# Soft mixture of experts on Trainium2: keeping the slot pass's logits in DRAM for the combine

## The chip, the cores and the metric

One core of one Trainium2 chip runs the whole program. The metric is the device time in microseconds (us) of one execution. Data are float32 unless a row says bf16.

## What is computed

The reference is a network of four residual layers over x (16 batches, 512 positions, 256 features). The first three (an attention over a context of 1601 keys, a low-rank feed-forward layer, a second attention) stand in the kernel's first stage, which the change leaves alone. The fourth is a soft mixture of 64 experts with 32 slots each, 2048 slots in all:

```python
def _L1_ffn_ref(x, phi, W, b):
    logits = jnp.einsum('bmd,dnp->bmnp', x, phi)
    dispatch = jax.nn.softmax(logits, axis=0)
    combine = jax.nn.softmax(logits.reshape(bsz, m, n * p), axis=-1).reshape(bsz, m, n, p)
    slots = jnp.einsum('bmd,bmnp->bnpd', x, dispatch)
    y = jnp.einsum('bnpd,nde->bnpe', slots, W) + b[None, :, None, :]
    out = jnp.einsum('bnpd,bmnp->bmd', y, combine)
    return out
x = x + _L1_ffn_ref(_layernorm(x, axis=-1), ...)
```

The same logits are used twice: through a softmax over the 16 batches (dispatch) and through a softmax over the 2048 slots (combine).

## The kernel before

`stage_two` runs after the first stage. It is written by hand for each engine: each has its list of instructions, and semaphores join them. The 2048 slots are cut into 16 slabs of 128 slots (4 experts), the 512 positions of a batch into 4 groups of 128 (QT). All of x, normalised and transposed (`xT`, 8 MB), and `phi` (2 MB) lie in SBUF.

**The slot pass.** A tile n is one slab and one group of positions, for all 16 batches: 128 positions on the partitions, 16 x 128 logits along the row, 1 MB, in one of 10 buffers of `disp`. There are 64 tiles.
- TensorE: `logits` (L1479) multiplies a quarter of a tile (4 batches) into a PSUM bank; ScalarE's `evacuate` (L1581) copies it to `disp`.
- VectorE: `front(n)` takes the maximum over the batches as a tree (L1651, L1654 to L1658), the maximum of each row (L1652), and subtracts the former in place (L1660); ScalarE's `exponent` (L1587) follows, then `back(n)` on VectorE sums and inverts (L1669 to L1679), and POOL's `normalise` (L1460) multiplies.
- TensorE: `slots(s, p)` (L1494) multiplies two batches of x (`xnb`, two buffers, loaded by SP one batch at a time at L1425) by the weights of slab s; ScalarE copies the result out (L1593), `experts` (L1509) multiplies by the experts' matrices, VectorE's `add_bias` (L1686) adds the bias, and ScalarE's queue stores two batches of y (L1599) to `y_d` in DRAM.

The order on TensorE is one step g for a slab and a pair of batches, 128 steps: a quarter of a tile of logits, `slots`, another quarter, `experts` of the step before. The logits run 6 tiles ahead, so the last 12 steps have none. Every slab SP also loads the next experts' weights (L1412, L1415) behind the load of batch 6.

**The combine.** The logits are not kept. For a block of one batch b and one slab c, 256 blocks in all, TensorE computes them again, this time with slots on the partitions and the 512 positions along the row:

```python
for k in range(2):
    mm(o, phi[:, k, c * P:(c + 1) * P], xT[:, b, k, :], start=(k == 0), stop=False)
mm(o, ones3[:, :], shift[b % 2], start=False, stop=True).then_inc(c_mm, 1)
```

The third matmul subtracts each position's maximum, given as three bf16 rows (`shift_rows`, L1535). ScalarE takes the exponential from PSUM (L1630), and two blocks later TensorE's `combine` (L1557) multiplies four groups of 128 positions by y, with a column of ones behind the 256 of y, which sums the denominators. After 16 slabs of a batch VectorE's `finish` takes four reciprocals (L1732) and adds the result to the residual (L1737), and ScalarE's queue stores the batch (L1637). SP loads y of a batch (L1431, 2 MB, in pieces of 1 KB) and its residual (L1435).

Of the kernel before, what the change touches and what calls it, by code (L numbers as in the profile page):

```python
# [12 lines left out]
P = 128  # L13
B, S, D = 16, 512, 256
NK = 1601
QT = S // P
# [1304 lines left out]
def stage_two(nc, w, x3_d, xn_d, xnT_d, y_d, out, ident, psum):  # L1321
# [9 lines left out]
    LAG = 2  # L1331

    with ExitStack() as st:
# [18 lines left out]
        ngr = sb("ngr", [P, QT, B])  # L1352
        ngp = sb("ngp", [P, QT, B, 3], BF16)
        ones3 = sb("ones3", [P, P], BF16)
        identb = sb("identb2", [P, P], BF16)

        flat = disp[:, :, :, :].rearrange("p r b n -> p (r b n)")
        TILE = B * SL
        ya = [flat[:, 4 * TILE:4 * TILE + NSL * (D + 1)].rearrange("p (c e) -> p c e", e=D + 1),
              flat[:, 4 * TILE + NSL * (D + 1):4 * TILE + 2 * NSL * (D + 1)].rearrange("p (c e) -> p c e", e=D + 1)]  # L1360
        x3 = [flat[:, 9 * TILE + i * QT * D:9 * TILE + (i + 1) * QT * D].rearrange("p (t d) -> p t d", d=D)
              for i in range(2)]
        ex = [flat[:, i * S:(i + 1) * S] for i in range(4)]
        shift = [flat[:, TILE + i * 256:TILE + (i + 1) * 256].bitcast(BF16) for i in range(2)]
        rc = sb("rc", [P, 2, QT])
# [21 lines left out]
        ng_ready = sem("ng_ready")  # L1387
        ng_tr = sem("ng_tr")
        shift_zero = sem("shift_zero")
        shift_ready = sem("shift_ready")  # L1390
        ones_made = sem("ones_made")
        y_in = [sem(f"y_in{i}") for i in range(2)]
        x3_in = [sem(f"x3_in{i}") for i in range(2)]
        c_mm = sem("c_mm")
        c_exp = sem("c_exp")
        o_mm = sem("o_mm")
        o_rc = sem("o_rc")
        o_ready = sem("o_ready")
        o_stored = [sem(f"o_stored{i}") for i in range(2)]
# [3 lines left out]
        def _(sp):  # L1403
# [14 lines left out]

            parameters(0)
# [10 lines left out]
            def values(b, c0, c1):  # L1430
                sp.dma_start(ya[b % 2][:, c0:c1, 0:D],  # L1431
                             y_d[b].rearrange("(p c) e -> p c e", c=NSL)[:, c0:c1, :]).then_inc(y_in[b % 2], 16)

            def residual(b):
                sp.dma_start(x3[b % 2], x3_d[b].rearrange("(p t) d -> p t d", t=QT)).then_inc(x3_in[b % 2], 16)  # L1435

            sp.wait_ge(ones_made, 1)
            for i in range(2):
                sp.wait_ge(y_stored[i], 16 * PAIRS * NSL // 2)
            for b in range(B):  # L1440
                if b >= 2:
                    sp.wait_ge(o_mm, NSL * (b - 1))
                values(b, 0, NSL)
                if b >= 2:
                    sp.wait_ge(o_stored[b % 2], 16 * (b // 2))
                residual(b)
            for i in range(2):
                sp.wait_ge(o_stored[i], 16 * (B // 2))

        @block.gpsimd  # L1450
        def _(pool):
            pool.memset(ones3[:, :], 0.0).then_inc(made, 1)
            pool.wait_ge(made, 1)
            pool.memset(ones3[0:3, :], 1.0).then_inc(made, 1)
            pool.tensor_copy(identb[:, :], ident[:, :]).then_inc(made, 1)

# [10 lines left out]
        def _(pe):  # L1467
# [61 lines left out]
            def shift_rows(b):  # L1529
                if b == 0:  # L1530
                    pe.wait_ge(ng_ready, 1)
                    pe.wait_ge(made, 3)
                tb = bank[3 - b % 2].bitcast(BF16)
                for t in range(QT):
                    last = nc.tensor.transpose(tb[0:3, t * P:(t + 1) * P], ngp[:, t, b, :], identb[:, :])  # L1535
                last.then_inc(ng_tr, 1)

            def scores(b, c):
                n = b * NSL + c
                if n >= 2:  # L1540
                    pe.wait_ge(c_exp, n - 1)
                o = bank[n % 2]
                for k in range(2):
                    mm(o, phi[:, k, c * P:(c + 1) * P], xT[:, b, k, :], start=(k == 0), stop=False)  # L1544
                if c == 0:
                    pe.wait_ge(shift_ready, b + 1)
                mm(o, ones3[:, :], shift[b % 2], start=False, stop=True).then_inc(c_mm, 1)  # L1547

            def combine(b, e):
                n = b * NSL + e  # L1550
                if e == 0:
                    pe.wait_ge(y_in[b % 2], 16 * (b // 2 + 1))
                    if b >= 1:
                        pe.wait_ge(o_ready, b)
                pe.wait_ge(c_exp, n + 1)
                for t in range(QT):
                    last = mm(bank[4 + t][:, 0:D + 1], ex[n % 4][:, t * P:(t + 1) * P], ya[b % 2][:, e, :],  # L1557
                              start=(e == 0), stop=(e == NSL - 1))
# [3 lines left out]
            shift_rows(0)  # L1562
            for n in range(B * NSL + LAG):
# [214 lines left out]
```

## Time and profile before

| what | value |
|---|---|
| device time, 3 runs | 6866.95 us median (6860.8 to 6872.46) |
| device time of the profiled execution | 6864.03 us |
| its span, from first to last instruction | 6862.2 us |
| first stage | up to 4646.84 us, where `xT` begins to load |
| load of phi and xT, then the slot pass | 4646.84 to about 5897 us |
| combine | about 5897 to 6862 us |
| busy: PE, DVE, ACT, POOL | 92%, 51%, 48%, 35% of the span |
| granted TensorE clock, mean | 0.975 of 2.4 GHz |
| DRAM traffic | 387.94 MB read, 151.28 MB written |

PE is TensorE, DVE VectorE, ACT ScalarE, PEld TensorE's weight loads, which run beside the matmuls. A float32 matmul stands as two records, a transpose or a bf16 matmul as one. The records' durations overlap, so the pace of a stretch is read from start to start. "SPq" and "ACTq" are the DMA queues of SP and ScalarE.

### The profile page before, as it was taken

Reading aid. Unit: us, or ns where it says so; the run is one execution under the profiler, and the core shown is the slowest. Engines: PE = TensorE matmul, PEld = TensorE weight load, DVE = VectorE, ACT = ScalarE, POOL = GpSimd, SP = SyncE. Lnnn points to the kernel's source line nnn. Section 1 sums busy time; section 2 is a strip of 40 time slices with the busy share of each in tenths; the row PEclk is TensorE's granted clock in tenths of the full one; section 3 lists DMA queues with packets and bytes.
Section 4 is the critical chain, followed back from the end, with each engine's and each line's share of the span. In section 5 each row is a group of like instructions: output and inputs, shape, how many; then the busy total and the mean of one; then the engine's idle time right before and its main releaser. Section 6 shows DMA issues by size and latency. Waiting matters only on the chain. (4 is left out here: it accounts for less than half of the span.)

```text
span 6862.2 us, 93027 instructions
## 1 busy us (share of the span) xinstructions
PE 6307.0 (92%) x35933; PEld 3091.1 (45%) x35933; DVE 3514.3 (51%) x6804; ACT 3263.7 (48%) x6001; POOL 2408.1 (35%) x2689
## 2 busy tenths in 40 slices
PE   3799999999999999999999999966999999999999
PEld 1223333333333333333333333226888888666666
DVE  3565665665656656656656566516666666000000
ACT  1366666666666666666666666522222222111111
POOL 4226436346355264363463552342222222000000
PEclk9799999999999999999999999968999999999999
DMA  2442332432432423314324324003444444311110
GB/s 64 77 76 57 67 76 56 73 69 63 76 71 55 84 57 66 78 55 73 69 63 76 70 53 75 6 16 135 157 167 154 158 162 163 121 56 56 49 56 31
DMA packets 364938, 546.09 MB, mean 80 GB/s; under 512 B 59824, under 2 KB 281984, under 8 KB 364240
## 3 DMA queue, kind: packets, MB, share of 16 engines
q1 hardware_dynamic: 321232, 498.18, 30.0%
q10 hardware_dynamic: 43264, 41.95, 1.8%
q8 instruction: 285, 4.67, 0.3%
q14 instruction: 157, 1.29, 0.1%
HBM read 387.94 MB, written 151.28 MB: 79 GB/s over the span
## 5 line engine op out<-in xcount | busy, mean ns | idle before, releaser
L1193 DVE TENSOR_REDUCE mx<-psum 128x1 f32<-128x401 f32 x4096 | 2212.9, 570 | 1615.7 <-PE psum L767 1606.6
L1038 ACT ACTIVATE probs<-psum 128x512 f32<-128x512 f32 (+1 forms) x3328 | 1910.6, 599 | 910.4 <-PE psum L789 907.3
L767 PE MATMUL psum<-kst,qst 96*128 96x401 bf16 x4096 | 1356.6, 343 | 192.5 <-DVE mx L1193 149.6
L789 PE MATMUL psum<-qst,kst 99*128 99x512 bf16 (+1 forms) x3328 | 1286.0, 387 | 49.9 <-ACT probs L1038 44.8
L800 PE MATMUL psum<-probs,vaug 128*17 128x512 f32 x6656 | 886.8, 605 | 0.0
L789 PEld LDWEIGHTS psum<-qst,kst 99*128 99x128 bf16 (+1 forms) x3328 | 328.8, 99 | 1178.5 <-ACT probs L1038 748.9
L767 PEld LDWEIGHTS psum<-kst,qst 96*128 96x128 bf16 x4096 | 402.7, 98 | 962.8 <-DVE mx L1193 756.3
L1460 POOL TENSOR_TENSOR disp<-disp,rz 128x2048 f32<-128x2048 f32 x64 | 294.7, 4605 | 905.5 <-DVE rz L1679 905.5
L1479 PE MATMUL psum<-phi,xT 128*128 128x128 f32 x4096 | 511.0, 279 | 39.1 <-DMA xT<-xnT_scratch 31.8
L1630 ACT ACTIVATE disp<-psum 128x512 f32<-128x512 f32 x256 | 152.8, 597 | 807.6 <-PE psum L1547 807.6
L1479 PEld LDWEIGHTS psum<-phi,xT 128*128 128x128 f32 x4096 | 479.0, 193 | 86.8 <-issue 79.1
L1494 PE MATMUL psum<-disp,xnb 128*128 128x128 f32 x4096 | 486.0, 276 | 27.0 <-POOL disp L1460 18.8
L1557 PE MATMUL psum<-disp 128*128 128x257 f32 x2048 | 487.5, 381 | 6.3 <-issue 4.0
L1494 PEld LDWEIGHTS psum<-disp,xnb 128*128 128x128 f32 x4096 | 470.6, 193 | 35.6 <-POOL disp L1460 19.6
L1544 PE MATMUL psum<-xT,phi 128*128 128x512 f32 x1024 | 485.1, 596 | 0.0
L1557 PEld LDWEIGHTS psum<-disp 128*128 128x128 f32 x2048 | 388.3, 190 | 143.5 <-issue 93.0
L644 POOL TENSOR_SCALAR rs<-mv 128x4 f32<-128x4 f32 x48 | 11.1, 231 | 1242.4 <-DVE mv L1245 1242.4
L725 PE MATMUL psum<-wkv,cT 128*128 128x512 f32 (+1 forms) x832 | 406.6, 611 | 12.7 <-ACT sq L1006 7.2
L1581 ACT ACTIVATE disp<-psum 128x512 f32<-128x512 f32 x256 | 152.1, 597 | 461.4 <-PE psum L1479 461.4
L1732 DVE RECIPROCAL rc<-psum 128x1 f32<-128x1 f32 x64 | 5.8, 153 | 599.9 <-PE psum L1557 599.9
L1686 DVE TENSOR_TENSOR ysb<-psum,be 128x512 f32<-128x512 f32 x128 | 88.5, 691 | 422.2 <-PE psum L1509 422.2
L1593 ACT ACTIVATE slT<-psum 128x512 f32<-128x512 f32 x128 | 76.4, 597 | 407.7 <-PE psum L1494 407.7
(197 smaller groups left out, 7556.2 us busy)
## 6 DMA issues: line engine op xcount, KB each, us to landing
xnb<-xn_scratch SPq DMA_DIRECT2D x256, 512.0 KB, 3.6
kst<-k_planes SPq DMA_DIRECT2D x384, 200.1 KB, 8.8
k_planes<-pl SPq DMA_DIRECT2D x96, 384.0 KB, 3.2
y_scratch<-ysb ACTq DMA_DIRECT2D x128, 256.0 KB, 3.3
disp<-y_scratch SPq DMA_DIRECT2D x16, 2048.0 KB, 9.2
vaug<-v_scratch SPq DMA_DIRECT2D x64, 442.0 KB, 4.6
v_scratch<-vst SPq DMA_DIRECT2D x48, 544.0 KB, 3.1
cin<-in_ctx SPq DMA_DIRECT2D x48, 512.0 KB, 3.8
```

Of the source, the lines that this page charges most:

```text
L725: last = mm(hb[0:m, :], cT[:, n % 2, k, a * P:a * P + m], wkv[:, k, :], start=(k == 0), stop=(k == 1))
L767: mm(to[:, 0:PW], qst[g][0:NP, j, t * P:(t + 1) * P], kst[g][0:NP, j, k0:k0 + PW], start=True, stop=True).then_inc(m_full, 1)
L789: mm(bank[S_BANK[n % 2]][0:m, :], kst[g][0:NR, j, c * P:c * P + m], qst[g][0:NR, j, :], start=True, stop=True).then_inc(s_full, 1)
L800: last = mm(bank[V_BANK][32 * j:32 * j + HV, :], vaug[0:m, g % 2, c, HV * j:HV * (j + 1)], probs[0:m, 4 * (k % 2) + j, :], start=(c == 0), ...
L1038: fn(probs[0:m, 4 * (k % 2) + j, :], bank[S_BANK[j % 2]][0:m, :], ACT.Exp, scale=float(HD) ** 0.5).then_inc(s_exp, 1)
L1193: v.tensor_reduce(mx[:, n % 2, u // 4, u % 4:u % 4 + 1], bank[M_BANK[r % 2]][:, 0:PW], AX.X, ALU.max).then_inc(m_free, 1)
L1460: pool.tensor_tensor(d, d, rz[:, n % 2, None, :].broadcast_to((P, B, SL)), ALU.mult).then_inc(normed, 1)
L1479: last = mm(bank[u % 4][:, a * SL:(a + 1) * SL], xT[:, 4 * q + a, k, t * P:(t + 1) * P], phi[:, k, s * SL:(s + 1) * SL], start=(k == 0), s ...
L1494: last = mm(bank[4 + n % 2][:, (2 * a + h) * SL:(2 * a + h + 1) * SL], xnb[:, a, t, h * P:(h + 1) * P], disp[:, (QT * s + t) % RING, b, :] ...
L1544: mm(o, phi[:, k, c * P:(c + 1) * P], xT[:, b, k, :], start=(k == 0), stop=False)
L1557: last = mm(bank[4 + t][:, 0:D + 1], ex[n % 4][:, t * P:(t + 1) * P], ya[b % 2][:, e, :], start=(e == 0), stop=(e == NSL - 1))
L1630: fn(ex[n % 4], bank[n % 2], ACT.Exp).then_inc(c_exp, 1)
```

## The change

Each tile's logits are stored to DRAM (`lg_d`, 64 MB in all) as soon as they are evacuated, pieces of 1 KB (128 slots of two neighbouring batches). VectorE's subtraction, which overwrites them, waits for that store. The combine works on a pair of batches, 32 blocks, in four units of 2 MB (4 slabs x 2 batches, rows of 4 KB). SP loads a unit into the place of `xT`, four buffers; the first two units go out in the last slab behind the load of batch 4, and 15/16 of batch 0's y behind that of batch 10. ScalarE exponentiates a unit in place, 8 instructions of 128 x 512 that subtract the maximum through the bias and sum the row (`accum_out`). TensorE transposes 4 groups of 128 x 128 of a block into a bank, VectorE copies the bank to `exT`, and two blocks later TensorE multiplies by y, now 256 columns wide. The two `scores` matmuls, the `ones3` matmul and the `shift` rows are gone. y and residuals have four buffers each; y is loaded in rows of 16 KB.

```diff
@@ SP
+            def logits_back(u):
+                if u >= 4:
+                    sp.wait_ge(tr_mm, 8 * (u - 3))
+                sp.dma_start(lgb[:, u % 4, :, :, :, :]..., lg_d[u // 4]...).then_inc(lg_in[u % 4], 16)
...
+                    if s == NSL - 1 and b == 4:
+                        sp.wait_ge(l_mm, 4 * TILES)
+                        for i in range(2):
+                            sp.wait_ge(lg_stored[i], 16 * (TILES // 2))
+                        logits_back(0)
+                        logits_back(1)
+                    if s == NSL - 1 and b == 10:
+                        for i in range(2):
+                            sp.wait_ge(y_stored[i], 16 * PAIRS * (NSL - 1) // 2)
+                        values(0, 0, NSL - 1)
+            for u in range(2, 4):
+                logits_back(u)
+            sp.wait_ge(sl_mm, B * NSL)
+            for i in range(4):
+                residual(i)
             for i in range(2):
                 sp.wait_ge(y_stored[i], 16 * PAIRS * NSL // 2)
+            values(0, NSL - 1, NSL)
+            for b in range(1, 4):
                 values(b, 0, NSL)
+            for p in range(PAIRS):
+                for h in range(4):
+                    if 4 * p + h + 4 < UNITS:
+                        logits_back(4 * p + h + 4)
+                if p + 2 < PAIRS:
+                    sp.wait_ge(o_mm, 2 * NSL * (p + 1))
+                    for b in (2 * p + 4, 2 * p + 5):
+                        values(b, 0, NSL)
+                    for b in (2 * p + 4, 2 * p + 5):
+                        sp.wait_ge(o_stored[b % 4], 16 * (b // 4))
+                        residual(b)
@@ TensorE
-            def scores(b, c):
...
-                for k in range(2):
-                    mm(o, phi[:, k, c * P:(c + 1) * P], xT[:, b, k, :], start=(k == 0), stop=False)
-                mm(o, ones3[:, :], shift[b % 2], start=False, stop=True).then_inc(c_mm, 1)
+            def transpose_back(n):
+                u, i, a = n // 8, n % 8 // 2, n % 2
+                if n % 8 < 2:
+                    pe.wait_ge(c_exp, 2 * QT * u + QT * (a + 1))
+                if n >= 4:
+                    pe.wait_ge(ex_ready, n - 3)
+                for t in range(QT):
+                    last = nc.tensor.transpose(bank[n % 4][:, t * P:(t + 1) * P], lgb[:, u % 4, t, i, a, :], ident[:, :])
+                last.then_inc(tr_mm, 1)
+            def combine(n):
+                p, e, a = n // (2 * NSL), n % (2 * NSL) // 2, n % 2
+                b = 2 * p + a
+                pe.wait_ge(ex_ready, n + 1)
+                if e == 0:
+                    pe.wait_ge(y_in[b % 4], 16 * (b // 4 + 1 + (b % 4 == 0)))
                 for t in range(QT):
+                    if e == 0 and a == 0 and p >= 1:
+                        pe.wait_ge(o_ready, 2 * QT * (p - 1) + 2 * t + 2)
+                    last = mm(bank[4 + t][:, a * D:(a + 1) * D], exT[n % 4][:, t * P:(t + 1) * P], ya[b % 4][:, e, :],
+                              start=(e == 0 and a == 0), stop=(e == NSL - 1), skip_group_check=True)
                 last.then_inc(o_mm, 1)
@@ ScalarE
+            def store_logits(n):
+                act.wait_ge(l_copied, 4 * n + 4)
+                if n >= 2:
+                    act.wait_ge(lg_stored[n % 2], 16 * (n // 2))
+                act.dma_start(lg_d[:, n % QT, :, n // QT, :]..., disp[:, n % RING, :, :]...).then_inc(lg_stored[n % 2], 16)
+            def weights(u):
...
+                        fn(d, d, ACT.Exp, bias=nm[:, t, b:b + 1], accum_out=sums[:, b % 4, t, h:h + 1]).then_inc(c_exp, 1)
+            for p in range(PAIRS):
+                for h in range(4):
+                    if 4 * p + h + 4 < UNITS:
+                        weights(4 * p + h + 4)
+                store_out(2 * p)
+                store_out(2 * p + 1)
@@ VectorE, front(n)
                 dve.wait_ge(front_step, base + 5)
+                dve.wait_ge(lg_stored[n % 2], 16 * (n // 2 + 1))
                 v.tensor_tensor(d, d, bm[:, None, :].broadcast_to((P, B, SL)), ALU.subtract).then_inc(shifted, 1)
@@ VectorE, combine
+            def copy_back(n):
+                dve.wait_ge(tr_mm, n + 1)
+                if n >= 4:
+                    dve.wait_ge(o_mm, n - 3)
+                v.tensor_copy(exT[n % 4], bank[n % 4]).then_inc(ex_ready, 1)
...
+            for n in range(BLOCKS + LAG):
+                if n < BLOCKS:
+                    copy_back(n)
+                if n % (2 * NSL) == 28 and n < BLOCKS:
+                    denominators(n // (2 * NSL))
+                if n >= 2 * NSL and n % (2 * NSL) == 1:
+                    finish(n // (2 * NSL) - 1)
```

TensorE in the middle of the combine, before (two blocks):

```order
L1544 MATMUL psum<-xT,phi 128x512 x2
L1547 MATMUL psum<-disp,ones 128x512
L1557 MATMUL psum<-disp 128x257 x4
L1544 MATMUL psum<-xT,phi 128x512 x2
L1547 MATMUL psum<-disp,ones 128x512
L1557 MATMUL psum<-disp 128x257 x4
```

and with the change (two blocks; `xT` is here the place of the logits that came back):

```order
L1562 MATMUL psum<-ident,xT 128x128 x4
L1574 MATMUL psum<-disp 128x256 x4
L1562 MATMUL psum<-ident,xT 128x128 x4
L1574 MATMUL psum<-disp 128x256 x4
```

Three matmuls of 512 columns have left each block, four transposes of 128 columns have come.

SP's queue over the last slab and the start of the combine, with the change (the loads into `xT` are logits, those of `y_scratch` are y, those of `x_scratch` residuals, 512 KB each):

```order
L1442 DMA xnb<-xn_scratch 128x1024 [waits sl_mm] x14
L1425 DMA xT<-logit_scratch 128x4x1024 [waits lg_stored1,lg_stored0,l_mm]
L1425 DMA xT<-logit_scratch 128x4x1024
L1442 DMA xnb<-xn_scratch 128x1024 [waits sl_mm] x6
L1430 DMA phi<-y_scratch 128x3840 [waits y_stored1,y_stored0]
L1442 DMA xnb<-xn_scratch 128x1024 [waits sl_mm] x5
L1425 DMA xT<-logit_scratch 128x4x1024 x2
L1434 DMA xnb<-x_scratch 128x1024 [waits sl_mm]
L1434 DMA xnb<-x_scratch 128x1024
L1434 DMA disp<-x_scratch 128x1024 x2
L1430 DMA phi<-y_scratch 128x256 [waits y_stored1,y_stored0]
L1430 DMA disp<-y_scratch 128x4096 x3
```

and the same stretch before:

```order
L1425 DMA xnb<-xn_scratch 128x1024 [waits sl_mm] x25
L1431 DMA disp<-y_scratch 128x16x256 [waits y_stored1,y_stored0,ones_made]
L1435 DMA disp<-x_scratch 128x1024
L1431 DMA disp<-y_scratch 128x16x256
L1435 DMA disp<-x_scratch 128x1024
```

Loads of 2 MB now stand between the loads of `xnb` of the last slab, and eight loads ahead of the last three of y.

VectorE at the border of two pairs, with the change: the eight additions to the residual stand between two copies of a block.

```order
L1749 COPY disp<-psum 128x512 [waits o_mm,tr_mm] x4
L1766 SCALAR_TENSOR_TENSOR xnb<-psum,rc,xnb 128x256 [waits x3_in1,x3_in0,o_mm]
L1766 SCALAR_TENSOR_TENSOR xnb<-psum,rc,xnb 128x256 x7
L1749 COPY disp<-psum 128x512 [waits o_mm,tr_mm] x27
```

## Rows read from the trace of the kernel before

**Rows 1.** The page's costliest groups: the two float32 matmuls of the combine.
```profile
L1557 PE MATMUL psum<-disp 128*128 128x257 f32 x2048 | 487.5, 381 | 6.3 <-issue 4.0
L1544 PE MATMUL psum<-xT,phi 128*128 128x512 f32 x1024 | 485.1, 596 | 0.0
```
**Rows 2.** Busy time by stretch (us, then PE, PEld, DVE, ACT, POOL; clock, DMA, GB/s): combine.
```profile
5907.00:6860.00 953.00, 945.75 (x3373) 607.38 (x3373) 38.55 (x143) 151.06 (x253) 0.00 (x0) 1.00 0.16 50
```
**Rows 3.** Timeline of PE in the combine (start, us, engine, line): one block.
```profile
6301.91 1.88 PE L1544 MATMUL psum<-xT,phi 128*128 128x512 f32 x4
6303.63 0.38 PE L1547 MATMUL psum<-disp,ones 128*128 128x512 bf16 x1
6303.85 1.90 PE L1557 MATMUL psum<-disp 128*128 128x257 f32 x8
6305.58 1.88 PE L1544 MATMUL psum<-xT,phi 128*128 128x512 f32 x4
```
**Rows 4.** Timeline of PE in the first stage: four float32 transposes, and what follows, twice.
```profile
3005.52 0.66 PE L748 MATMUL psum<-ident,kraw 128*128 128x128 f32 x4
3006.01 0.38 PE L789 MATMUL psum<-qst,kst 99*128 99x512 bf16 x1
...
3009.43 0.60 PE L748 MATMUL psum<-ident,kraw 128*128 128x128 f32 x4
3009.86 0.34 PE L767 MATMUL psum<-kst,qst 96*128 96x401 bf16 x1
```
**Rows 5.** Timeline of the slot pass, all engines, from one evacuation to a slab's start.
```profile
5163.27 0.60 ACT L1581 ACTIVATE disp<-psum 128x512 f32<-128x512 f32 x1 [1.19 <-PE psum L1479]
...
5170.60 2.29 DVE L1660 TENSOR_TENSOR disp<-disp,bm 128x2048 f32<-128x2048 f32 x1
...
5174.37 0.69 DVE L1686 TENSOR_TENSOR ysb<-psum,be 128x512 f32<-128x512 f32 x1 [1.40 <-PE psum L1509]
...
5178.77 4.54 POOL L1460 TENSOR_TENSOR disp<-disp,rz 128x2048 f32<-128x2048 f32 x1 [13.86 <-DVE rz L1679]
...
5185.33 3.74 PE L1494 MATMUL psum<-disp,xnb 128*128 128x128 f32 x32
```
**Rows 6.** Waits, 4740 to 5840 us: us in total, times, longest.
```profile
PE psum L1494 <- POOL disp L1460: 15.8, 1, 15.8
PE psum L1494 <- DMA xnb<-xn_scratch: 6.3, 9, 1.9
```
**Rows 7.** DMA, 4740 to 5840 us: ScalarE's queue (packets, MB, share); its stores, us to landing.
```profile
q10 hardware_dynamic: 31824, 30.68, 8.0%
...
y_scratch<-ysb ACTq DMA_DIRECT2D x118, 256.0 KB, 3.2
```
**Rows 8.** The chain of waits (start, us): the last of xT's load, 4 x 2 MB.
```profile
4646.84 24.39 DMA xT<-xnT_scratch
```
**Rows 9.** Timeline, all engines: from the last slab to the first combine.
```profile
5882.97 2.05 PE L1494 MATMUL psum<-disp,xnb 128*128 128x128 f32 x16 [0.41 <-DMA xnb<-xn_scratch]
...
5890.95 3.66 PE L1509 MATMUL psum<-we,slT 128*32 128x256 f32 x64
...
5897.61 0.62 SPq L1431 DMA_DIRECT2D disp<-y_scratch  x1
...
5906.86 3.02 PE L1557 MATMUL psum<-disp 128*128 128x257 f32 x8 [2.37 <-DMA disp<-y_scratch]
```
**Rows 10.** Busy time by stretch: the first combine matmuls.
```profile
5906.90:5909.70 2.80, 2.80 (x9) 2.26 (x10) 0.00 (x0) 0.00 (x0) 0.00 (x0) 0.64 1.08 353
```
**Rows 11.** Timeline: VectorE after one batch, and TensorE's last matmuls.
```profile
6264.84 1.66 DVE L1737 SCALAR_TENSOR_TENSOR disp<-psum,rc,disp 128x256 f32<-128x256 f32 x4
...
6851.35 5.37 PE L1557 MATMUL psum<-disp 128*128 128x257 f32 x24
```
**Rows 12.** Groups by line: a copy out of PSUM; the reading of an accumulated sum.
```profile
L1272 DVE COPY g_a<-psum 32x512 f32<-32x512 f32 x1 | 0.7, 678 | 1.1 <-PE psum L889 1.1
...
L1020 ACT ACTIVATION_READ_ACCUMULATOR kv1s<-psum,bkv 32x1 f32 x56 | 10.4, 185 | 0.0
```

More of the change, by code:

```diff
@@ L1450, in _ @@
+            for i in range(4):
+                sp.wait_ge(o_stored[i], 16 * (B // 4))
         @block.gpsimd
         def _(pool):
[L1452 to L1455, printed above, removed]
             def normalise(n):
@@ L1559, in combine @@
                 last.then_inc(o_mm, 1)
             pe.wait_ge(y_ready, PAIRS * NSL)
-            shift_rows(0)
-            for n in range(B * NSL + LAG):
-                b, c = n // NSL, n % NSL
-                if n < B * NSL:
-                    if c == NSL // 2 and b + 1 < B:
-                        shift_rows(b + 1)
-                    scores(b, c)
+            pe.wait_ge(l_copied, 4 * TILES)
+            for n in range(BLOCKS + LAG):
+                if n < BLOCKS:
+                    transpose_back(n)
@@ L1569, in _ @@
                 if n >= LAG:
-                    combine((n - LAG) // NSL, (n - LAG) % NSL)
+                    combine(n - LAG)
         @block.scalar
@@ L1587, in exponent @@
                 fn(d, d, ACT.Exp).then_inc(exped, 1)
+            def weights(u):
+                p, h = u // 4, u % 4
+                act.wait_ge(lg_in[u % 4], 16 * (u // 4 + 1))
+                if u == 0:
+                    act.wait_ge(nm_ready, 1)
+                if h == 0 and p >= 2:
+                    act.wait_ge(o_den, p - 1)
+                for a in range(2):
+                    b = 2 * p + a
+                    for t in range(QT):
+                        d = lgb[:, u % 4, t, :, a, :]
+                        fn(d, d, ACT.Exp, bias=nm[:, t, b:b + 1], accum_out=sums[:, b % 4, t, h:h + 1]).then_inc(c_exp, 1)
             def slots_out(g):
@@ L1604, in _ @@
                     evacuate(n, q)
+                store_logits(n)
                 if n >= 1:
@@ L1622, in _, with store_out @@
             store_y(NSL * PAIRS - 1)
-            for n in range(B * NSL):
-                act.wait_ge(c_mm, n + 1)
-                if n == 0:
-                    act.wait_ge(sl_mm, B * NSL)
-                if n >= 4:
-                    act.wait_ge(o_mm, n - 3)
-                fn(ex[n % 4], bank[n % 2], ACT.Exp).then_inc(c_exp, 1)
-                b, c = n // NSL, n % NSL
-                if b >= 1 and c == 6:
-                    act.wait_ge(o_ready, b)
-                    act.dma_start(out[b - 1].rearrange("(t p) d -> p t d", p=P), x3[(b - 1) % 2])\
-                        .then_inc(o_stored[(b - 1) % 2], 16)
-            act.wait_ge(o_ready, B)
-            act.dma_start(out[B - 1].rearrange("(t p) d -> p t d", p=P), x3[(B - 1) % 2])\
-                .then_inc(o_stored[(B - 1) % 2], 16)
+            def store_out(b):
+                act.wait_ge(o_ready, 2 * QT * (b // 2 + 1))
+                act.dma_start(out[b].rearrange("(t p) d -> p t d", p=P), x3[b % 4]).then_inc(o_stored[b % 4], 16)
+            for u in range(1, 4):
+                weights(u)
+            for p in range(PAIRS):
[4 more added lines that the diff above has]
+                store_out(2 * p + 1)
         @block.vector
@@ new lines, in finish @@
+            def finish(p):
+                dve.wait_ge(o_mm, 2 * NSL * (p + 1))
+                for b in (2 * p, 2 * p + 1):
+                    dve.wait_ge(x3_in[b % 4], 16 * (b // 4 + 1))
+                for t in range(QT):
+                    for a in range(2):
+                        i = (2 * p + a) % 4
+                        v.scalar_tensor_tensor(out=x3[i][:, t, :], in0=bank[4 + t][:, a * D:(a + 1) * D],
+                                               scalar=rc[:, i, t:t + 1], in1=x3[i][:, t, :],
+                                               op0=ALU.mult, op1=ALU.add).then_inc(o_ready, 1)
```

143 lines of the change are left out of this document (50 added, 93 removed).

## The prediction, made blind

> **What bounds the kernel now.** I read the groups by cost first, then the busy time by stretch, then the timeline of one block, of one slab's start and of the passage between the two passes, and last the waits and the DMA queues. TensorE is busy 945.75 of 953 us of the combine, at the full clock (1.00, the 2.4 GHz level) and with the DMA engines at 0.16 [rows 2]: nothing but TensorE's own work sets this stretch, and its other engines (DVE 38.55, ACT 151.06 us) could do much more. The two large groups are the recomputed scores, 485.1 us, and the product with y, 487.5 us [rows 1]. The slot pass is bound by TensorE as well: between 4740 and 5840 us it waits 15.8 us once for POOL, at the first slab, and 6.3 us in 9 pieces for loads of x [rows 6]. So what is removed from TensorE in the combine shortens the run, and what is added to the slot pass costs only where it breaks a cover.
>
> **The combine, block by block.** A block takes 3.67 us from start to start (6301.91 to 6305.58): scores 1.72, the bf16 matmul 0.22, the product with y 1.73 [rows 3]. The product stays, with 256 columns in place of 257: 1.72 us. The first two go, 1.94 us. Four float32 transposes come. In the first stage four of them take 0.49 and 0.43 us from their start to the next instruction's [rows 4]; I take 0.46. The trace shows no transpose right before a float32 product, whose weight loads are longer; the nearest bound from above is the slot pass, whose matmuls of the same 128 columns, as two records each, take 3.74 / 16 = 0.23 us [rows 5], four of them 0.93. I take 0.46, because that row is the same instruction on the same shape, and keep 0.93 as a rival. A block is then 2.18 us.
>
> Is that pace covered by the other engines? VectorE copies one bank per block; a copy of 512 columns out of PSUM takes 0.68 us [rows 12]. ScalarE's exponential over 512 columns takes 0.60 us, as its copy does [rows 5], with up to 0.19 us for reading the sum [rows 12]: 0.79 us. Both fit in 2.18 us. DMA: a pair of batches reads 8.4 MB of logits, 4.2 of y, 1.05 of residuals and writes 1.05, 14.7 MB in 32 blocks (70 us), or 210 GB/s. Loads in rows of 4 KB ran at 8.4 MB in 24.39 us [rows 8], 344 GB/s, so this is 43 us of transfer in 70. Four units are buffered, and SP asks for one as soon as the transposes of the unit before it in that buffer are done, three units (52 us) ahead of its use. SP does stop at the end of each pair for y's buffers and for the stores of the results, which stand on ScalarE's queue behind the last unit's exponentials: some 8 us of load, 6 of exponentials, 3 of store, so 17 us, and the next unit can't be asked for before 8 blocks (17 us) anyway. I cost that at nothing.
>
> **Borders of two batches.** Now VectorE does eight additions between two pairs where TensorE waits for bank after bank. Four take 1.66 us [rows 11], so the fourth bank is free 3.3 us after the last product, where TensorE, which has one block of transposes (0.46) and three quarters of a product (1.3) to do by then, wants it at 1.8: 1.5 us of stall, 7 times, 11 us.
>
> **The stores in the slot pass.** 64 stores of 1024 packets of 1 KB. The same form exists: y is stored in 1 KB pieces, 256 KB in 3.2 us, and ScalarE's queue used 0.080 x 1100 us x 16 engines for 31824 packets, 44 ns each [rows 7]. So 16 packets per engine are 0.7 us and 2.5 us are fixed; 64 packets are 2.8, and a store is 5.3 us, with up to 2.2 us more for two loads of x at the same time: 7.5 us. VectorE's subtraction now waits for it. The last evacuation ends at 5163.87 and the subtraction starts at 5170.60 [rows 5], 6.7 us later, so it starts 0.8 us late. Behind it on VectorE stands the bias addition, which waits 1.40 us for TensorE, and behind that the sums whose normalisation on POOL ends at 5183.31, 2.0 us ahead of the slab's first matmul [rows 5]. The cover is 3.4 us past the 6.7, so a store may take 10.1 us before TensorE feels it. Nothing for the wait; 0.5 us for each of 15 slabs where store, weights and loads of x collide, since TensorE already waits there for x [rows 6]: 7 us. Issuing a store takes about half a microsecond on ScalarE, which is idle half the time.
>
> The trace shows no store whose pieces lie 8 MB apart, as these do from pair to pair; y's, 2 MB apart, are the nearest. The Trainium skill, "DMA: Bandwidth & Descriptors", section "Latency and other measured facts", speaks against the change here: rows whose pitch is 4 or 8 MiB went at 103 GB/s where 512 KiB gave 207. By that page 1 MB is an estimated 10.2 us plus what is fixed, some 12.7 us, 2.6 us past the cover in each of 15 slabs, and the sum would be 39 us longer; no run here shows it.
>
> **The last slab and the start of the combine.** Four of SP's lines are moved past each other. Two units (4.2 MB, 12.2 us at 344 GB/s) go out ahead of x's batch 5, whose load has no spare in the last slab (a wait of 0.41 us there already [rows 9]) but is asked for 3 us later: 9 us of stall. y of batch 0 (2 MB, 5.7 us) ahead of batch 11: 3 us. Then, from the end of batch 13's slots at 5885.02 [rows 9], two units (12.2 us), four residuals (2.1 MB, 6.1), the rest of y of batch 0, and y of batch 1 (6.1) stand in one queue; the second block's product needs the last of these: 5885.0 + 24.9 + 2.5 fixed = 5912.5. Before, the first product started at 5906.86 [rows 9].
>
> **The sum**, on the profiled execution's 6864.03 us. The last product ended at 6851.35 + 5.37 = 6856.72 [rows 11]. Now 255 products (438.6 us) and 252 blocks of transposes (115.9) follow 5912.5: 6467.0, or -389.7. Borders +11, last slab +12, collisions +7. After a pause the matmuls run slower: the first product after the 2.37 us wait took 2.81 us in place of 1.73, at clock 0.64, between the 1.2 and 2.4 GHz levels [rows 9, 10]; nine pauses at half of that 1.1 us, +5. After the last product four more additions and one more store, less four reciprocals: +1.5. Together -353, so 6511 us. The median of the runs is 3 us above the profiled execution: **6514 us**. Between the small terms at nothing (with transposes at 0.43) and at double, this case spans 6483 to 6550.
>
> **The rivals.**
> A store slower than y's: if a packet took three times 44 ns, the store would be 8.4 + 2.5 + 2.2 = 13.1 us, 3.0 past the cover, 45 us in 15 slabs: 6559; at 15.8 us 6600. For it: 8 MB steps. Against: the same 1 KB packets in rows 7.
> Transposes at the pace of two records: +0.47 x 256 = 120 us, 6634. Against: rows 4.
> The combine bound by its loads: were 14.7 MB per pair to go at the slot pass's 160 GB/s, a pair would take 92 us in place of 71, 7 x 21 = 147: 6661. Against: that rate was what was asked for, and 344 was reached [rows 8].
> Slower than before: TensorE's clock stays at the 1.2 GHz level through the combine, because a fifth of its time is transposes and each border is a pause. Each block doubles, 256 x 2.18 = 558 us: 7072 us. It decides once 353 / 558 = 63% of the blocks run so. Against: the product with y fills four fifths of the time, and the clock came back to 1.00 within the next blocks after the drop [rows 2, 10]. The Trainium skill, "TensorE: Matmul & The Clock Gate", Part 4, says that transposes do not count as busy for the clock gate in the way matmuls do.
>
> **How the numbers follow.** The forecast 0.74, the slow store 0.11, two-record transposes 0.05, loads 0.05, the clock 0.04, and 0.01 for gain and losses that cancel. The range leaves out the last four: 6483 to 6600. About 0.2% (14 us) can be told from no change: faster 0.95, same 0.01, slower 0.04.
>
> **What would show it.** Blocks of 2.18 us from start to start at clock 1.00; no wait of TensorE in the combine but some 1.5 us at seven borders; stores landing in 5 to 8 us, and POOL's group still hardly waited for; a wait of about 9 us for x in the last slab; the second product at about 5925, with the earlier terms. Wrong: blocks above 2.3 us, POOL or DMA as what TensorE waits for at each slab, clock under 0.9, or the wait for y or logits at the start of each pair.

## The result, and the profile after

| | before | after |
|---|---|---|
| median | 6864.85 us (4 runs) | 6524.49 us (4 runs, 6520.53 to 6529.98) |
| ratio to before | | 0.9504 (95% interval 0.9488 to 0.9519) |
| span of the profiled execution | 6862.2 us | 6518.7 us |
| DRAM read / written | 387.94 / 151.28 MB | 455.04 / 218.39 MB |

The forecast was 6514 us in a range of 6483 to 6600. The run is 340 us shorter; 67 MB more are written and 67 MB more are read for it. From the start of `xT`'s load to the end of the span it is 1876 us where it was 2215.

The timeline of TensorE in the combine, one block (start us, us, engine, line), answers to [rows 3]:

```profile
6164.18 1.89 PE L1574 MATMUL psum<-disp 128*128 128x256 f32 x8
6165.91 0.60 PE L1562 MATMUL psum<-ident,xT 128*128 128x128 f32 x4
6166.34 1.89 PE L1574 MATMUL psum<-disp 128*128 128x256 f32 x8
```

From 6164.18 to 6166.34 is 2.16 us, where a block took 3.67. Four transposes take 0.43 us from their start to the product's, the lower of the two values of [rows 4].

Busy time by stretch in the combine (stretch, its length, then PE, PEld, DVE, ACT, POOL; clock, DMA, GB/s), as [rows 2]:

```profile
5960.00:6480.00 520.00, 514.30 (x2811) 445.70 (x2810) 185.97 (x305) 161.02 (x448) 0.00 (x0) 1.00 0.51 186
```

TensorE is still busy 99% of the stretch, at the 2.4 GHz level (1.00), with the DMA engines at half (0.51).

The border between two pairs of batches, TensorE and then VectorE:

```profile
6155.39 0.60 PE L1562 MATMUL psum<-ident,xT 128*128 128x128 f32 x4
6156.61 2.96 PE L1574 MATMUL psum<-disp 128*128 128x256 f32 x8 [0.62 <-DVE xnb L1766]
6159.41 0.60 PE L1562 MATMUL psum<-ident,xT 128*128 128x128 f32 x4
```

```profile
6155.59 3.23 DVE L1766 SCALAR_TENSOR_TENSOR xnb<-psum,rc,xnb 128x256 f32<-128x256 f32 x8 [1.04 <-PE psum L1574]
```

That block takes 4.02 us, 1.86 more than the others. Most of the stall does not stand as idle time: the product is drawn out from 1.73 to 2.80 us because it waits for one bank after another (`combine` has a wait for `o_ready` ahead of each of its four groups).

The DMA view of the slot pass, 4740 to 5850 us, answers to [rows 7]:

```profile
q10 hardware_dynamic: 92144, 91.50, 24.8%
...
logit_scratch<-disp ACTq DMA_DIRECT2D x58, 1024.0 KB, 5.3
y_scratch<-ysb ACTq DMA_DIRECT2D x118, 256.0 KB, 5.3
```

A store of 1 MB lands after 5.3 us at the median, the figure that was worked out from y's stores; the 64 stores took 4.7 to 6.9 us each; a packet took 0.248 x 1110 us x 16 / 92144 = 48 ns, against 44. y's stores, which share ScalarE's queue with the logits', went from 3.2 to 5.3 us.

Waits, 4640 to 5850 us (total us, times, longest), answer to [rows 6]:

```profile
PE psum L1520 <- POOL disp L1486: 15.8, 1, 15.8
PE psum L1520 <- DMA xnb<-xn_scratch: 13.7, 10, 2.4
...
DVE disp L1697 <- DMA logit_scratch<-disp: 0.3, 1, 0.3
```

VectorE hardly waits for a store and TensorE waits for POOL as before. TensorE's waits for x have doubled, from 6.3 us in 9 to 13.7 in 10. The longest of them, in the timeline of SP's queue and TensorE:

```profile
4832.74 0.32 SPq L1442 DMA_DIRECT2D xnb<-xn_scratch  x1
4833.11 0.93 SPq L1415 DMA_DIRECT2D we<-in_L_ffn_W  x1
4834.08 3.19 SPq L1418 DMA_DIRECT2D be<-in_L_ffn_b  x4
...
4837.31 10.59 SPq L1442 DMA_DIRECT2D xnb<-xn_scratch  x3
...
4844.31 3.23 PE L1520 MATMUL psum<-disp,xnb 128*128 128x128 f32 x16 [2.40 <-DMA xnb<-xn_scratch]
```

Issuing the weights and the four small loads of the biases keeps SP busy from 4833.11 to 4837.27; the next load of x is issued late, stands behind 1 MB, and shares the engines with y's store. This issuing is not typical: over the 15 slabs the five issues take 44 us in all, and took 40 in the kernel before. Behind this wait the matmuls are slow as well: 16 of them take 3.23 us where they take 2.05, and the granted clock from 4844.3 to 4850.0 is 0.70. Three of the ten waits (2.40, 2.32 and 1.90 us) are followed by such a stretch; the other seven are not, for example:

```profile
5665.51 2.05 PE L1520 MATMUL psum<-disp,xnb 128*128 128x128 f32 x16 [1.69 <-DMA xnb<-xn_scratch]
```

The last slab and the start of the combine, all engines, answer to [rows 9]:

```profile
5852.69 6.69 PE L1520 MATMUL psum<-disp,xnb 128*128 128x128 f32 x32 [2.99 <-POOL disp L1486]
...
5867.28 2.05 PE L1520 MATMUL psum<-disp,xnb 128*128 128x128 f32 x16
...
5880.28 3.78 PE L1520 MATMUL psum<-disp,xnb 128*128 128x128 f32 x16 [10.96 <-DMA xnb<-xn_scratch]
...
5906.05 3.40 PE L1520 MATMUL psum<-disp,xnb 128*128 128x128 f32 x16 [4.68 <-DMA xnb<-xn_scratch]
...
5921.34 3.66 PE L1535 MATMUL psum<-we,slT 128*32 128x256 f32 x64
...
5926.84 0.69 DVE L1723 TENSOR_TENSOR ysb<-psum,be 128x512 f32<-128x512 f32 x1 [8.76 <-DMA y_scratch<-ysb]
...
5930.90 2.82 PE L1562 MATMUL psum<-ident,xT 128*128 128x128 f32 x12 [5.90 <-DVE ysb L1723]
...
5941.20 3.37 PE L1574 MATMUL psum<-phi,disp 128*128 128x256 f32 x8 [7.49 <-DMA phi<-y_scratch]
...
5946.30 1.97 PE L1574 MATMUL psum<-disp 128*128 128x256 f32 x8 [1.29 <-DMA disp<-y_scratch]
```

The two early loads cost waits of 10.96 and 4.68 us, and after each the matmuls run slower: 3.78 and 3.40 us for what takes 2.05, at a granted clock of 0.50, the 1.2 GHz level (5880.3 to 5884.0), and 0.57 (5906.0 to 5909.4). The slab's first group is slow too, 6.69 us at clock 0.54 behind a wait of 2.99 us for POOL; in the kernel before, the same group took 3.84 us behind a wait of 3.07.

Then a step appears that the prediction has not: VectorE's last two bias additions wait 8.76 and 2.62 us for older stores of y, so that TensorE waits for VectorE, and SP, which waits for the last store, issues y's loads late. Two things lie behind it. The stores land late, beside the loads of logits: 9.3 and 8.6 us after their issue. And they are issued late: the additions of the two pairs in question ended at 5912.32 and 5918.08, but in ScalarE's list their stores stand behind the copy of a later pair's slots, and go out at 5917.53 and 5921.45. What the second costs was not tried.

### The profile page after: what moved, and what is told of

Its sections match the earlier page's. It is cut to its first block and busy times, and to the rows that moved or that the text cites. A ratio compares the mean times of both kernels' runs of the same rounds, so it can differ in the third digit from the quotient of the medians.

```text
span 6518.7 us, 93097 instructions
## 1 busy us (share of the span) xinstructions
PE 5927.6 (91%) x35613; PEld 2981.1 (46%) x35613; DVE 3677.9 (56%) x6989; ACT 3300.6 (51%) x6257; POOL 2407.3 (37%) x2686
## 3 DMA queue, kind: packets, MB, share of 16 engines
HBM read 455.04 MB, written 218.39 MB: 103 GB/s over the span
## 5 line engine op out<-in xcount | busy, mean ns | idle before, releaser
L1749 DVE COPY disp<-psum 128x512 f32<-128x512 f32 x256 | 176.9, 691 | 366.4 <-PE psum L1562 366.3
L1574 PE MATMUL psum<-disp 128*128 128x256 f32 x1536 | 366.6, 380 | 4.6 <-DVE xnb L1766 2.5
L1595 ACT ACTIVATE disp<-psum 128x512 f32<-128x512 f32 x256 | 152.1, 597 | 430.6 <-PE psum L1505 430.3
L1621 ACT ACTIVATE xT<-xT,nm 128x512 f32<-128x512 f32 x256 | 181.0, 708 | 347.7 <-DMA xT<-logit_scratch 338.7
L1574 PEld LDWEIGHTS psum<-disp 128*128 128x128 f32 x1536 | 276.0, 190 | 39.6 <-DVE xnb L1766 5.6
L1535 PE MATMUL psum<-we,slT 128*32 128x256 f32 x4096 | 248.6, 383 | 0.0
```

The costliest lines, as they stand in the source:

```text
L1535: last = mm(bank[6 + n % 2][32 * j:32 * j + 32, a * D:(a + 1) * D], slT[:, n % 2, a, k, 32 * j:32 * j + 32], we[:, s % 2, j, k, :], start= ...
L1574: last = mm(bank[4 + t][:, a * D:(a + 1) * D], exT[n % 4][:, t * P:(t + 1) * P], ya[b % 4][:, e, :], start=(e == 0 and a == 0), stop=(e == ...
L1621: fn(d, d, ACT.Exp, bias=nm[:, t, b:b + 1], accum_out=sums[:, b % 4, t, h:h + 1]).then_inc(c_exp, 1)
```

## The experiments

Each was compared with the kernel before on the same chip; the changed kernel had 6524.49 us (ratio 0.9504) in its own comparison. The kernel before took 6865 to 6875 us in these comparisons, so steps of a few us between two variants are uncertain. The first stage alone, which no variant touches, ended between 4641 and 4656 us in the traces; where a trace is to show a small step, the time from the start of `xT`'s load to the end of the span is given (2215 us before, 1876 changed). Where one execution is all there is, the text says so.

**The stores alone.** The kernel before with `store_logits` and VectorE's wait added, nothing read back.

```diff
+                store_logits(n)
+                dve.wait_ge(lg_stored[n % 2], 16 * (n // 2 + 1))
```

> The kernel before, with one part of the change alone: every tile's logits are stored and the subtraction waits for the store; nothing reads them back, and the combine is the old one. Theory (stores are covered, collisions cost): the stores land in some 5.3 us, the subtraction has 6.7 us, so nobody waits for a store; TensorE's waits for x at the loads of the experts' weights grow from 6.3 us to about 14, and the run is 7 to 15 us longer than before (about 6872 to 6880). Rival (the stores hold the chain of the slot pass through VectorE's wait): VectorE waits for stores in many tiles, TensorE for POOL at the slabs, and the run is 45 us or more longer.

Measured: 6888.89 us against 6873.4, ratio 1.0021 (1.0011 to 1.0031), so 14 us (8 to 21) longer. In the traces `xT`'s load to the last slab's first matmul takes 1211.5 us against 1197.3. TensorE's waits for x, 4740 to 5840 us:

```profile
PE psum L1496 <- DMA xnb<-xn_scratch: 13.0, 10, 2.1
```

VectorE waited twice for a store, 0.5 us together, from 4640 to 5850 us. The theory holds: the stores are covered, and the cost comes with x's loads, whose waits grew from 6.3 to 13.0 us.

**Each tile stored twice.**

```diff
+                act.dma_start(lg2_d[:, n % QT, :, n // QT, :]..., disp[:, n % RING, :, :]...).then_inc(lg2_stored[n % 2], 16)
+                dve.wait_ge(lg2_stored[n % 2], 16 * (n // 2 + 1))
```

> The changed kernel with each tile's logits stored twice, to two places, and the subtraction waiting for both. Theory (a cover of 6.7 us up to VectorE's first wait and 10.1 us up to TensorE): 64 packets per engine more, 2.8 us, so both have landed after about 8.1 to 9.5 us; VectorE now waits 1 to 3 us for stores in most tiles, TensorE still hardly for POOL at the slabs, and the run is 0 to 25 us longer than the changed kernel's, what there is coming from x's loads. Rival (every microsecond past 6.7 reaches TensorE): 2 us in each of 58 tiles, over 100 us.

Measured: 6780.27 us, one execution, 256 us longer than the changed kernel, ten times the most that the theory gave. The DMA view, 4740 to 5900 us:

```profile
q10 hardware_dynamic: 130409, 130.32, 49.8%
...
logit_scratch<-disp ACTq DMA_DIRECT2D x100, 1024.0 KB, 11.3
```

A packet now takes 0.498 x 1160 x 16 / 130409 = 71 ns, and the second store of a tile lands after 12.6 us at the median. The waits, 4640 to 6100 us:

```profile
DVE disp L1704 <- DMA logit_scratch<-disp: 366.2, 60, 8.3
...
PE psum L1522 <- DMA xnb<-xn_scratch: 185.8, 73, 7.9
...
PE psum L1522 <- POOL disp L1488: 19.3, 8, 17.5
```

The rival's mechanism was not right either: TensorE waits for POOL as little as ever, and 186 us for x's loads, 172 more than the changed kernel up to its last slab. The rest is mostly clock: from 4740 to 6080 us it is 0.94 where it was 0.99, and TensorE's records take 103 ns in the mean against 97, an estimated 70 us. VectorE waited 366 us for stores, and the cover behind it up to TensorE held; the loads of x, which share the engines with the stores (5.0 us to landing at the median in place of 3.8), had none.

**The second store in another form, and both with a padded distance.** Two kernels, compared with the one above: the second store in whole rows of 8 KB (`lg2_d` as 64 tiles x 128 x 2048), and both stores in 1 KB pieces with 8 MB + 36 KB from pair to pair.

```diff
-lg_d = nc.dram_tensor("logit_scratch", (PAIRS, QT, P, NSL, 2 * SL), ...)
+lg_d = nc.dram_tensor("logit_scratch", (PAIRS, QT * P * NSL * 2 * SL + 9 * 1024), ...)[:, 0:QT * P * NSL * 2 * SL]...
```

> The kernel that stores each tile twice (6780 us), with the second store in rows of 8 KB, one per partition and one tile behind the other in DRAM, in place of pieces of 1 KB whose pairs lie 8 MB apart. The question is why a second megabyte cost so much more than the 2.8 us of the theory. Theory A (the pieces or their places slow a sustained store): the second store takes about 3 us more than the first and the run falls to 6525 to 6600 us. Theory B (DRAM or the queues take writes of any form at such a rate no faster, about 250 GB/s): the run stays above 6700 us.

> The kernel that stores each tile twice (6780 us), both stores in pieces of 1 KB as there, but with the distance from pair to pair 8 MB + 36 KB in place of 8 MB. Theory A1 (places a power of two apart collide in DRAM): the stores speed up, and the run falls below 6650 us. Theory A2 (the size of a piece) or B (the rate of writes of any form): no change, 6760 to 6800 us. The Trainium skill, DMA: Bandwidth and Descriptors, section Latency and other measured facts, says that a few KiB of padding bring the full rate back at pitches of 4 MiB.

Measured: 6571.11 and 6578.64 us, one execution each. With the padding alone, 4740 to 5900 us:

```profile
q10 hardware_dynamic: 151920, 151.80, 42.3%
...
logit_scratch<-disp ACTq DMA_DIRECT2D x116, 1024.0 KB, 6.7
```

52 ns per packet in place of 71, the second store lands after 8.0 us in place of 12.6, and 202 of the 256 us are gone with no change in the size of a piece. So it is where the pieces lie in DRAM, not their size or the rate of writes as such, that slows the doubled stores. Two explanations are left that no run separates: the distance of 8 MB from pair to pair, and the distance between the two copies of a tile, whose stores are issued 0.4 us apart; the padding, which makes each copy's array 288 KB longer, can change both, and so can the second store in rows. The Trainium skill, "DMA: Bandwidth & Descriptors", "Latency and other measured facts", has a rule for the first, measured on copies within DRAM; the runs agree with its direction and with the cure, while the loss in a packet is 71 against 52 ns here, less than the page's factor of two.

**The padding on the changed kernel.**

> The changed kernel (each tile stored once, as it is) with the distance from pair to pair in the logits' place in DRAM 8 MB + 36 KB in place of 8 MB. Theory (the power of two costs only where stores are long enough to pile up; one megabyte in 18.4 us lands in 5.3 us, inside the 6.7 us of cover): the stores land up to 0.5 us earlier, TensorE's waits for x before the last slab (13.7 us) shrink by a few, and the run is the same within 5 us. Rival (the added cost of the slot pass is this collision in DRAM): TensorE's waits for x fall back to the 6.3 us of before, and the run is 7 to 15 us shorter.

Measured: 6521.89 us (ratio 0.9493, 0.9480 to 0.9506), not told apart from the run without: 3 us less by the medians, 7 by the ratios, whose intervals overlap. Stores land after 5.0 us in place of 5.3. TensorE's waits for x from 4740 to 5840 us are 12.5 us after 13.7, not the 6.3 of the rival, and that decides: the added waits are not this distance. With one store in 18.4 us it costs at most a few us.

**The experts' weights in pieces.**

```diff
-                    if b == 6 and s + 1 < NSL:
-                        parameters(s + 1)
+                    if 6 <= b < 6 + 2 * EN and s + 1 < NSL:
+                        parameters(s + 1, b - 6)
...
```

`parameters(s, piece)` loads the matrices of one of the four experts, or the biases of one.

> The changed kernel with the next slab's experts' weights and biases loaded in eight pieces, one behind each of the loads of x of batches 6 to 13, in place of one of 1 MB and four small ones behind that of batch 6. Theory (the added cost of the slot pass is the collision of these loads with x's and the stores): TensorE's waits for x before the last slab, 13.7 us, go to under 3, and the run is 10 to 14 us shorter. Rival (the stores alone slow x's loads): no change, within 3 us.

Measured: 6508.78 us (ratio 0.9478, 0.9466 to 0.9491), 16 us shorter. The waits from 4740 to 5840 us:

```profile
PE psum L1524 <- DMA xnb<-xn_scratch: 3.2, 2, 3.1
```

From 13.7 to 3.2 us of waiting, and of the three slow stretches before the last slab one is left; a little more was gained than the 10 to 14 us expected. The theory holds: the slot pass's added cost comes at the weights' loads, and with them cut up the slot pass with its stores is no longer than it was without stores. From the first slots to the last slab's first matmul the traces have 1100.6 us before, 1113.7 changed and 1096.9 here, so the cut also takes away waits that the kernel before had. It was not tried on the kernel before, and the size of a load and the number of issues in a row were changed together.

**The early loads behind the last load of x.**

```diff
-                    if s == NSL - 1 and b == 4:
+                    if s == NSL - 1 and b == 15:
```

and batch 0's y behind them in place of behind batch 10. ScalarE's exponentials of the first unit move behind the slot pass as well.

> The changed kernel with the early loads (two units of logits, 15/16 of batch 0's y) moved behind the last load of x, and the first unit's exponentials behind the slot pass. Theory (a transfer ahead in the same queue costs its time wherever it stands, but here it is no longer on x's way): the waits for x of 11.0 and 4.7 us in the last slab go, but the combine's start now waits for all 6.1 MB more, 18 us of transfer behind the last x, so the first product comes 0 to 10 us later than in the changed kernel after all: the same time within 10 us. Rival (the early loads were pure loss): 15 us shorter.

Measured: 6521.09 us (6513.55 to 6531.85; ratio 0.9497, 0.9484 to 0.9510), no difference. From 5850 us on TensorE's waits for x fall from 17.0 to 5.7 us, but the first product now waits 14.7 us for y in place of 7.5, and the first transposes 10.5 us for the exponentials. The 6 MB cost their time on either side of the passage.

**Another order at the start of the combine.** Batch 1's y gets the buffer that is free first; units 2 and 3 and the residuals go behind the y of the first two batches.

```diff
-            for u in range(2, 4):
-                logits_back(u)
+            values(1, 0, NSL - 1)
...
             values(0, NSL - 1, NSL)
+            values(1, NSL - 1, NSL)
+            for u in range(2, 4):
+                logits_back(u)
...
```

> The changed kernel with SP's queue behind the last load of x in another order: first 15/16 of batch 1's y (its buffer moved to a place that is free by then), then the wait for the last stores of y and the last sixteenths of batches 0 and 1, and only then the units 2 and 3, the residuals and the y of batches 2 and 3. Theory (the start of the combine waits for what stands ahead in the queue, and the last stores of y for the same transfers): TensorE's waits of 5.9 and 7.5 us and VectorE's of 8.8 us for a store of y at the start of the combine shrink, and the run is 8 to 15 us shorter. Rival (the chain is that of the stores' own latency): 0 to 3 us.

Measured: 6513.88 us (ratio 0.9486, 0.9473 to 0.9499), 11 us shorter. The timeline:

```profile
5928.42 1.32 DVE L1725 TENSOR_TENSOR ysb<-psum,be 128x512 f32<-128x512 f32 x2 [8.71 <-DMA y_scratch<-ysb]
...
5929.79 1.53 PE L1564 MATMUL psum<-ident,xT 128*128 128x128 f32 x12 [3.25 <-DVE ysb L1725]
...
5934.31 3.02 PE L1576 MATMUL psum<-phi,disp 128*128 128x256 f32 x8 [2.99 <-DMA phi<-y_scratch]
```

Waits of 5.90 and 7.49 us became 3.25 and 2.99. In the chain of waits the last store of y, with no loads beside it, takes 2.28 us to land where it took 7.05. VectorE's wait for an older store of y stayed (8.71), with the 2 MB of batch 1's y in SP's queue in place of two units of logits, so that part of the expectation missed; this store is again issued late, at 5919.16, behind ScalarE's copy of a later pair.

**Both.**

> The changed kernel with both: the order of the queue at the start of the combine and the weights in pieces. If the two causes are separate, their gains add: 18 to 29 us shorter than the changed kernel, about 6496 to 6506 us. If one hides the other, no more than the larger of them.

Measured: 6495.68 us (6494.6 to 6503.24; ratio 0.9463, 0.9450 to 0.9475), 29 us shorter than the changed kernel. The gains of 16 and 11 add, within the noise.

**Both, padded.**

> The best kernel so far (weights in pieces and the start's order, 6496 us) with the padded distance as well. Theory: its slot pass has no waits for x left that a faster store could save, so it is the same as that kernel within 4 us. Rival: the padding adds its own gain of 7 us or more.

Measured: 6497.01 us (ratio 0.9454, 0.9441 to 0.9467), not told apart from the version without padding (0.9463); from the start of `xT`'s load to the end both take 1847 us in the traces. These two are the best versions found.

**The transposes twice.**

```diff
-                for t in range(QT):
+                for t in list(range(QT)) * 2:
```

> The changed kernel with every block's four transposes done twice in a row (same result). Theory (TensorE's own work sets the combine): a block grows by four transposes, 0.43 to 0.46 us, from 2.17 to about 2.61 us, so the run is 110 to 118 us longer. Rival (the combine is close to a bound by loads or VectorE, with TensorE's time partly cover): clearly less, 0 to 60 us.

Measured: 6626.17 us, one execution, 102 us longer than the changed kernel, below the 110 to 118 expected. The timeline of its TensorE, first in the middle, then at a border of two pairs:

```profile
6149.96 1.04 PE L1562 MATMUL psum<-ident,xT 128*128 128x128 f32 x8
6150.83 1.89 PE L1574 MATMUL psum<-disp 128*128 128x256 f32 x8
6152.56 1.04 PE L1562 MATMUL psum<-ident,xT 128*128 128x128 f32 x8
...
6024.81 1.04 PE L1562 MATMUL psum<-ident,xT 128*128 128x128 f32 x8
6026.03 2.96 PE L1574 MATMUL psum<-disp 128*128 128x256 f32 x8 [0.19 <-DVE xnb L1766]
6028.83 1.04 PE L1562 MATMUL psum<-ident,xT 128*128 128x128 f32 x8
```

A block is 2.60 us, 0.44 more, which would be 113 us in 256 blocks. But the block at a border takes 4.02 us (6024.81 to 6028.83), as it did without the second transposes: VectorE's additions set it, so the seven borders pay nothing. From the second product to the last one's end the traces have 671.2 us against 564.2, 107 more. TensorE sets the combine, and VectorE its borders.

**A second load ahead of each unit.** 2 MB more for each unit from the fifth on, into the place of the experts' weights.

```diff
+                    sp.dma_start(we[...], lg_d[u // 4]...).then_inc(spare_in, 16)
```

> The changed kernel with a second load of 2 MB, into a place that nobody reads, ahead of each unit of logits from the fifth on: 8.4 MB more per pair of batches, 23.1 MB in about 71 us, 325 GB/s, close to the 344 GB/s that the load of x reached. Theory (loads have a cover of three units): ScalarE waits less for its units' loads because they come later, TensorE starts to wait only where a unit comes after its block; the run is 0 to 50 us longer. Rival (the combine is already near its loads' limit): each byte more costs its whole time, 28 loads of 6.1 us, 170 us.

Measured: 6524.06 us, one execution, no longer at all. The DMA view, 5960 to 6480 us:

```profile
DMA packets 40434, 156.62 MB, mean 301 GB/s; under 512 B 1504, under 2 KB 8672, under 8 KB 38867
```

301 GB/s in place of 186 in this stretch, and TensorE waits for no load: the combine's loads have cover to spare.

## Why the prediction was right, point by point

- **A block of 2.18 us**: 2.16 to 2.17. The row of the first stage priced the transposes rightly (0.46 said, 0.43 measured), and the rival of two records each (0.93) fell. No weight load of the float32 product shows behind them.
- **VectorE, ScalarE and the loads as cover**: held. The exponential with its sum runs 0.71 us from start to start, not 0.79. SP's stop at the end of a pair cost nothing, and the doubled loads show how much was left.
- **Borders, 11 us**: 7 x 1.86 = 13. The wait for bank after bank is what was forecast; the stall is 0.4 us longer at each border.
- **A store of 5.3 us, covered**: right at both points; the slowest of the 64 took 6.9 us, inside the 7.5 that were allowed. Right with less cause was its margin: it was argued that a store may take 10.1 us because VectorE and POOL have that cover. The doubled stores show that x's loads suffer long before POOL does. The cover of the chain was read from the trace, that of the shared engines was not.
- **Collisions, 7 us**: too small. From the start of `xT`'s load to the last slab's first matmul the run went from 5844.14 - 4646.84 = 1197.3 us to 5852.69 - 4642.22 = 1210.5, 13 us more; the stores alone gave 14. The waits that were priced came as priced, 7.4 us more. What the sum lacks here is the slow clock behind three of them: the steps that follow (4844.31 to 4853.47, 5741.74 to 5750.89, 5830.41 to 5837.64) are 1.7, 1.7 and 1.3 us longer than the same steps at full clock, 5 us together. None of the nine waits of the kernel before, up to 1.9 us long, had such a stretch.
- **The last slab and the start**: the second product was to start 80.4 us after the last slab's first matmul (5912.5 + 12 - 5844.14); it started 5946.30 - 5852.69 = 93.6 us after it, 13 us more. Some 10 of them are in the last slab: up to the end of batch 13's slots it took 62.8 us (5852.69 to 5915.46) where it had taken 40.9 and 52.9 were said. Waits for x were 17.0 us against 1.5, so 15.5 more and not 12, and 6 us are slower matmuls (clock 0.82 in place of 1.00). The term for slow clock was mis-sized: 5 us for the whole run, where the last slab alone has 6 and the slot pass ahead of it 5. The other 3 us are in the passage, 30.8 us where 27.5 were said. There the mechanism was wrong although the time came near: the start does not wait for SP's queue alone, but for the last stores of y, beside loads on the other queue, and TensorE for VectorE through them. A better order of that queue gave 11 us.
- **The distance of 8 MB**, taken at nothing in the sum: right for this kernel by the padded run, and the 39 us that the prediction worked out from the Trainium skill's figure ("DMA: Bandwidth & Descriptors", "Latency and other measured facts") did not come. With the volume doubled, the places of the pieces cost about 200 us, by this distance or by the one between the copies.
- **The clock**: 1.00 from 5960 to 6480 us, after 0.83 in the first 29 us of the combine; the rival that ends above the time before fell. A fifth of TensorE's time in transposes (0.43 of 2.16 us) did not lower it. The Trainium skill, "TensorE: Matmul & The Clock Gate", Part 4, says that transposes do not count as busy in the same way; at this share the trace shows no effect of it.

The misses in the profiled execution: collisions +6, last slab and start +13 less the 5 for the clock, the end +1, combine -1, and a first stage 4.6 us shorter for no reason in the change: +9.7, where forecast (6511) and measured time (6520.53) differ by 9.5 us. The main term, the combine, was right in its mechanism and its size. That the total came within 10 us is in part luck: the first stage, which varied by 15 us between runs that leave it alone, happened to be short, and blocks of 2.16 in place of 2.18 us made up for the borders.

## What to carry to other kernels

Recomputing on a bound engine can be dearer than storing 64 MB and reading it back, if the transfers have queues and engines to spare: price it per block, bound engine against bound engine. When transfers are added, look for the load with the shortest cover that shares the engines, not only for who waits for the new transfer; here that was x's, and cutting a neighbour's 1 MB load into pieces won back about what the stores had cost (16 us and 14). Price a wait of TensorE above its length: after some of them the clock stays low for a few us. Where two phases meet, write down the order of the queue and put what is needed first at its head; moving the same bytes to the other side of the border gains nothing.

## What was not expected of the hardware

- The same stores in 1 KB pieces took 48 ns per packet at 1 MB per 18.4 us, 71 ns when each tile was stored twice, and 52 ns when it was stored twice with 36 KB added to the 8 MB between pairs. Where the pieces lie cost hardly anything at the single volume and about 200 us at the double one.
- A store of 256 KB in 1 KB pieces beside loads on the other queue took 9.3 us (issued at 5917.53, awaited until 5926.84), where the median was 3.2 in the slot pass of the kernel before [rows 7]. With 2 MB of loads issued ahead of it on the other queue in place of 4 it took 9.2; with none, the last store took 2.28 in place of 7.05.
- A wait for VectorE's banks shows as a drawn-out matmul group on TensorE (2.96 us for 1.89, 0.62 idle), so the idle column tells a third of such a stall.
- Waits of the same length need not end alike: 16 matmuls of the slots took 3.23 and 2.97 us behind waits of 2.40 and 2.32 us, at clock 0.70 and 0.68, and 2.05 us behind one of 1.69; behind waits of 2.99 and 3.07 us for POOL 32 of them took 6.69 and 3.84.
